# A four-layer graph network on one core: lane one-hots in two instructions, fewer TensorE signals, 15 of 98 blocks by products

## The reference

```python
m = relu(x @ Wp + bp)
agg = segment_max(m[src], dst, num_segments=n)     # 0 for a node without edges
h = x @ Ws + agg @ Wn + b                          # twice, then normalised
```

## Time and profile before

| | us |
|---|---|
| median of 3 runs (2958.58 to 2969.26) | 2963.22 |
| profiled execution | 2943.83 |
| its span | 2942.1 |

### The profile page before, as it was taken

How to read it: one execution, slowest core, us unless ns; L and a number is a source line. 1 busy time by engine, 2 the same in 40 slices (tenths; PEclk the granted TensorE clock), 3 DMA queues, 4 the chain that set the end, 5 groups by cost and what they waited for, 6 DMA issues and landing times. The chain is left out here.

```text
span 2942.1 us, 67814 instructions
## 1 busy us (share of the span) xinstructions
PE 2528.8 (86%) x26419; PEld 1892.6 (64%) x26419; DVE 1978.5 (67%) x6078; ACT 1227.1 (42%) x2920; POOL 1216.1 (41%) x1429
## 2 busy tenths in 40 slices
PE   6998999996778888747888888458799999999999
PEld 3444777773445544434455545337699999999999
DVE  7997999996788988726888888441244444444444
ACT  5997888884334444423444334330221111111110
POOL 2001999993677777634777777411000000000000
PEclk8998999997899998857999989659999999999999
DMA  6002000004343434342343444509700000000000
GB/s 197 1 1 91 12 13 12 12 12 112 93 111 107 121 109 114 104 88 68 108 120 108 112 112 137 160 8 321 239 2 2 2 2 2 2 2 2 2 2 18
DMA packets 163890, 208.87 MB, mean 71 GB/s; under 512 B 82829, under 2 KB 129194, under 8 KB 162896
## 3 DMA queue, kind: packets, MB, share of 16 engines
q1 hardware_dynamic: 135772, 165.27, 19.0%
q0 software_dynamic: 24256, 37.90, 5.3%
q10 hardware_dynamic: 3540, 1.30, 0.2%
HBM read 104.70 MB, written 102.05 MB: 70 GB/s over the span
## 5 line engine op out<-in xcount | busy, mean ns | idle before, releaser
L1782 POOL DMA_INDIRECT max_row<-table,max_src_rows x696 | 768.5, 1104 | 367.6 <-issue 240.4
L2349 PE MATMUL prop<-g,adj 128*128 128x192 f16 x9216 | 770.9, 246 | 7.1 <-PEq L2020 7.1
L2349 PEld LDWEIGHTS prop<-g,adj 128*128 128x128 f16 x9216 | 759.8, 98 | 14.9 <-issue 12.4
L1677 POOL TENSOR_SCALAR e<-e 128x512 f32<-128x512 f32 (+1 forms) x625 | 366.9, 606 | 244.4 <-ACT e L1665 228.0
L1691 DVE TENSOR_TENSOR e<-e,a_ps 128x1024 f32<-128x1024 f32 (+1 forms) x313 | 371.6, 1194 | 38.6 <-PE a_ps L1603 16.6
L2438 ACT ACTIVATE g<-prop_state 128x96 f16<-128x96 f32 (+1 forms) x375 | 106.0, 283 | 635.3 <-DVE prop_state L2406 635.3
L1665 ACT ACTIVATE e<-s_ps 128x512 f32<-128x512 f32 (+1 forms) x625 | 335.7, 585 | 62.3 <-PE o_ps L1615 38.8
L1822 PE MATMUL max_strip_ps<-max_key_hot,max_lane_w 128*128 128x400 f16 x1200 | 296.2, 361 | 72.4 <-issue 36.2
L2404 DVE SCALAR_TENSOR_TENSOR part<-prop,coef,prop_base 128x96 f32<-128x96 f32 x384 | 120.6, 314 | 312.9 <-PE prop L2349 225.5
L1875 DVE TENSOR_SCALAR max_lane_w<-iota,max_tables 128x128 f16<-128x128 f16 x1200 | 319.6, 313 | 0.0
L1812 PE MATMUL max_far<-adj 128*96 128x512 f16 x1100 | 285.9, 398 | 11.8 <-issue 11.6
(11 more groups left out here) (263 smaller groups left out, 3382.3 us busy)
## 6 DMA issues: line engine op xcount, KB each, us to landing
weights<-max_rows_w SPq DMA_DIRECT2D x52, 400.0 KB
rows_dram<-max_out SPq DMA_DIRECT2D x100, 192.0 KB
weights<-adj SPq DMA_DIRECT2D x48, 400.0 KB
ws_w<-weights SPq DMA_DIRECT2D x50, 384.0 KB, 5.2
rows_dram<-adj SPq DMA_DIRECT2D x96, 192.0 KB
ws_w<-weights SPq DMA_DIRECT2D x50, 288.0 KB, 4.5
max_row<-table,max_src_rows POOLq DMA_INDIRECT x696
ws_w<-weights SPq DMA_DIRECT2D x50, 128.0 KB, 2.8
```

What stands on the lines that cost most here:

```text
L1677: nc.gpsimd.tensor_scalar(e_tile(u), e_tile(u), math.exp(10.0), math.exp(-10.0), ALU.min, ALU.max).then_inc(clipped, 1)
L1782: nc.gpsimd.indirect_dma_start(row[i % RING][:, j, :], None, table_dram, bass.IndirectOffsetOnAxis(ap=src_rows[:, 4 * n + j:4 * n + j + 1] ...
L2349: return nc.tensor.matmul(sums(step, t), adj[:, k, t * P:(t + 1) * P], states[:, k, :], start=start and t % 2 == 0, stop=k == END - 1 and ...
```

## The change

- Far blocks: 15 of 98, every sixth, with 25 tiles over six steps and two PSUM banks in turn. `hot_used` is signalled after every second tile.
- `hots(n)`: the lane compare of all three windows is one `tensor_tensor` (384 columns), its product with both weight halves a second one (768 columns), with tables in which each lane and weight stands twice in 16 bit. Key and lane one-hots have two buffers; `hots_used` is signalled once a step.
- The low part of the strip: TensorE adds minus the high part to the strip in PSUM (`take_high`), and ScalarE copies what is left.
- `same` is loaded by SP straight from DRAM, spread over 96 partitions.
- `table` holds each row as 16-bit high and low halves (same bytes); `turn_rows` is 8 half-precision products in place of 4 float32 transposes. The layers store `table` from those halves.
- The tables are laid out by pass and loaded in one DMA.
- The count in `walk_adjacency` becomes a loop (not entered here).

```diff
-FAR = range(7, 88, 8)
+FAR = range(5, 92, 6)
@@ first_layer, second_layer: sync
-                sp.wait_ge(pooled, t + m)
-                sp.dma_start(node_view(table)[:, t:t + m, :], out[:, g % 2, 0:m, 0, :]).then_inc(stored[g % 2], 16)
                 sp.wait_ge(own_kept, t + m)
                 sp.dma_start(node_view(self_dram)[:, t:t + m, :], out[:, g % 2, 0:m, 1, :]).then_inc(stored[g % 2], 16)
+                sp.wait_ge(lo_kept, g + 1)
+                sp.dma_start(node_view(table)[:, t:t + m, :], parts[:, t:t + m, :, :].rearrange("p t a d -> p t (a d)").bitcast(F32)).then_inc(table_stored, 16)
@@ max_pass: tensor
                 for j in range(4):
-                    tr = nc.tensor.transpose(col_ps[i % 2][0:D, j * P:(j + 1) * P], row[i % RING][:, j, :], c.ident[:, :])
+                    for a in range(2):
+                        mm = nc.tensor.matmul(col_ps[i % 2][0:D, j * P:(j + 1) * P], row_parts[i % RING][:, j, a, :], c.ident16[:, :],
+                                              start=a == 0, stop=a == 1, skip_group_check=True)
...
+            def take_high(n):
+                pe.wait_ge(hi_kept, n + 1)
+                nc.tensor.matmul(strip_ps[n % 2][:, 0:KEYS], minus[:, :], strip_at(0, n).rearrange("p k d -> p d k"),
+                                 start=False, stop=True, skip_group_check=True).then_inc(hi_taken, 1)
...
-                if n >= 0 and n + SAME - 1 < NB:
-                    spread_same(n + SAME - 1)
-                for j, k in far_tiles(m):
-                    add_far(j, k)
+                tiles = far_tiles(m)
+                for i, (j, k) in enumerate(tiles):
+                    add_far(j, k, 2 if i % 2 == 1 else int(i == len(tiles) - 1))
+                if m < PARTS:
+                    take_high(m)
@@ max_pass: vector
             def hots(n):
+                steps = slice(WIN * n, WIN * (n + 1))
+                if n >= 1:
+                    dve.wait_ge(lanes_ready, n)
+                nc.vector.tensor_tensor(lane_hot.rearrange("p w (n a) -> p w n a", a=2),
+                                        c.iota16[:, 0:P].rearrange("p (n a) -> p n a", a=2).unsqueeze(1).to_broadcast([P, WIN, P // 2, 2]),
+                                        lanes[:, steps, :].unsqueeze(2).to_broadcast([P, WIN, P // 2, 2]), ALU.is_equal).then_inc(lanes_found, 1)
+                if n >= 2:
+                    dve.wait_ge(hots_used, n - 1)
                 for w in range(WIN):
...
-                    for h in range(2):
-                        one_hot = nc.vector.tensor_scalar(lane_w[:, w, h, :], c.iota16[:, 0:P], at(1), at(2 + h), ALU.is_equal, ALU.mult)
-                    one_hot.then_inc(hots_ready, 1)
+                    nc.vector.tensor_scalar(key_hot[n % 2][:, w, :], c.iota16[:, :], keys[:, WIN * n + w:WIN * n + w + 1], None, ALU.is_equal).then_inc(hots_ready, 1)
+                dve.wait_ge(lanes_found, n + 1)
+                nc.vector.tensor_tensor(lane_w[n % 2].rearrange("p h w (n a) -> p (h w) n a", a=2),
+                                        lane_hot.unsqueeze(1).to_broadcast([P, 2, WIN, P]),
+                                        weights[:, n, :, :].unsqueeze(2).to_broadcast([P, 2 * WIN, P // 2, 2]), ALU.mult).then_inc(lanes_ready, 1)
-            def low_part(n):
-                dve.wait_ge(hi_kept, n + 1)
-                nc.vector.tensor_tensor(strip_at(1, n), strip_ps[n % 2][:, 0:KEYS].rearrange("p (d k) -> p k d", d=GROUP),
-                                        strip_at(0, n), ALU.subtract).then_inc(lo_kept, 1)
@@ max_pass: scalar
+            def low_part(n):
+                act.wait_ge(hi_taken, n + 1)
+                nc.scalar.activation(strip_at(1, n), strip_ps[n % 2][:, 0:KEYS].rearrange("p (d k) -> p k d", d=GROUP), ACT.Copy).then_inc(lo_kept, 1)
@@ max_pass: sync
+            def load_same(n):
+                if n >= SAME:
+                    sp.wait_ge(scanned, n - SAME + 1)
+                at = n * BLK
+                sp.dma_start(same[n % SAME][:, :], same_dram[at:at + BLK].rearrange("(a e) -> a e", a=1).to_broadcast([D, BLK])).then_inc(same_loaded[n % SAME], 16)
```

More of the change, by code:

```diff
@@ L171, in first_layer @@
         loaded = [sem(f"loaded{g}") for g in range(len(GROUPS))]
-        stored = [sem(f"stored{i}") for i in range(2)]
+        stored, table_stored = [sem(f"stored{i}") for i in range(2)], sem("table_stored")
         w_loaded, x_stored, listed, ones_made, eps_made, d_step, x_ready, measured, std_ready, scaled = (
@@ L1700, with pass_tables, max_pass @@
 PIECES = (7, 6, 6, 6)
-def pass_tables(tables_dram, part):
-    return tables_dram.rearrange("p n (t q s) -> p n t q s", t=T, q=2)[:, :, :, part, :]
-def max_pass(nc, c, name, table_dram, src_rows, same_all, tables, rows_dram, weights_dram, part, adj, numbers, ids_dram, away_dram=None):
+PASS_STEPS = NSTEP // 2
+def pass_tables(tables):
+    keys, halves = tables[:, 0:PASS_STEPS], tables[:, PASS_STEPS:].bitcast(F16)
+    lanes = halves[:, 0:2 * PASS_STEPS].rearrange("p (s a) -> p s a", a=2)
+    weights = halves[:, 2 * PASS_STEPS:].rearrange("p (m s a) -> p m s a", s=2 * WIN, a=2)
+    return keys, lanes, weights
+def max_pass(nc, c, name, table_dram, src_rows, same_dram, tables, rows_dram, weights_dram, part, adj, numbers, minus, ids_dram, away_dram=None):
     SAME, LEAD, HOTS, OUTS = 4, 4, 6, 4
@@ L1726, in max_pass @@
         col_ps = [ps(f"col{i}") for i in range(2)]
-        back_ps, far_ps = ps("back"), ps("far")
-        same_ps = ps("same_ps")
+        back_ps, far_ps = ps("back"), [ps(f"far{i}") for i in range(2)]
         gathered = [c.gather_sem(f"{name}_gathered{i}") for i in range(RING)]
@@ L1731, in max_pass @@
         rows_stored = [sem(f"rows_stored{i}") for i in range(2)]
-        turned, cleared, scanned, spread, same_kept, back, kept, zero_out = (
-            sem("turned"), sem("cleared"), sem("scanned"), sem("spread"), sem("same_kept"),
-            sem("back"), sem("kept"), sem("zero_out"))
-        key_hot = sb("key_hot", [P, WIN, KEYS], F16)
-        lane_w = sb("lane_w", [P, WIN, 2, P], F16)
+        same_loaded = [sem(f"same_loaded{i}") for i in range(SAME)]
+        turned, cleared, scanned, back, kept, zero_out = (
+            sem("turned"), sem("cleared"), sem("scanned"), sem("back"), sem("kept"), sem("zero_out"))
+        key_hot = [sb(f"key_hot{i}", [P, WIN, KEYS], F16) for i in range(2)]
+        keys, lanes, weights = pass_tables(tables)
+        behind_out = more[:, T * P + 2 * 8 * D:]
+        lane_hot = behind_out[:, 0:WIN * P].rearrange("p (w n) -> p w n", w=WIN)
+        lane_w = [sb("lane_w", [P, 2, WIN, P], F16), behind_out[:, WIN * P:3 * WIN * P].rearrange("p (h w n) -> p h w n", h=2, w=WIN)]
+        lanes_found, lanes_ready = sem("lanes_found"), sem("lanes_ready")
         strip = sb("strip", [P, 2, T, 2, HALF], F16)
@@ L1757, in far_tiles @@
             for j, n in enumerate(FAR):
-                first, last = FAR[j - 1] + LEAD + 1 if j >= 1 else 1, n + LEAD - 1
+                first, last = FAR[j - 1] + LEAD if j >= 1 else 1, n + LEAD - 1
                 if first <= m <= last:
@@ L1843, in turn_back @@
                 tr.then_inc(back, 1)
-            for n in range(SAME - 1):
-                spread_same(n)
             for m in range(NB + LEAD):
```

146 lines of the change are left out of this document (75 added, 71 removed).

## The result

The changed kernel takes 2982.17 us (median of 7 runs, 2979.48 to 2989.74), the kernel before beside it 2967.16: the ratio is 1.0057, 95% interval 1.0041 to 1.0073. It is slower by about 15 us where 2918 was forecast. So differences between these two profiles overstate the change by about 20 us.

A forecast was written before the change was run, and what follows sets the result against it. GpSimd was taken as the bound, 490.7 of 524.2 us a pass. Own work -5 and signals -16.5 a pass, two passes -43, layer 2 -3, stores +1: -45, median 2918 us, range 2865 to 2990.

The forecast's parts named there:

- Signals: GpSimd's 33.5 us a pass of waiting for TensorE's late signals would shrink with fewer signals and doubled buffers: -16.5 us.
- Low part: Moved from VectorE to a strided TensorE product and ScalarE copy: TensorE +0.25 us a step, GpSimd -4 us a pass.
- Rival D: TensorE becomes the bound through the strided product and its wait for ScalarE, 5.5 us a step: 2979 us; chance 0.12.
- Rival A: Late TensorE signals stay, coming with full DMA engines, so only -5 us a pass: 2951 us; chance 0.20.
- Lane one-hots: On VectorE, one wide compare and one wide multiply would take 1.12 us a step in place of 1.6.
- Their weight on GpSimd: The wide lane operations on VectorE would slow GpSimd's gathers by +5 us a pass; removed lane instructions counted 0.
- Rival C: VectorE's two wide operations lock out GpSimd's gathers as far hots do: 3028 us; chance 0.10.
- Far hots: 100 more far one-hots a pass on VectorE would slow GpSimd's gathers by +14 us, between +5 and +20.8.
- GpSimd's own pass: GpSimd's gathers, issue and contention without waits would take 485.8 us a pass against 490.7.
- `same` by DMA: Loading by SP saves TensorE 0.3 us a step; the DMA share rises from 0.40 to about 0.47.
- Layer 2: The second layer would gain between 0 and 14.9 us from loading the tables in one DMA; taken -3.
- The build: A dozen more GpSimd table copies at the start, read only some 400 us later, would cost 0.

The follow-up runs named there:

- c4: Kernel before with `same` loaded by DMA alone, repeated on a late-signal chip: 0.9947 of before.
- e8: Changed kernel with 94 of 98 loads of `same` a pass left out, on a prompt chip (no late signals): 0.9866 of before.
- d1: Changed kernel with the low part back on VectorE and 11 far blocks for 15, on a prompt chip: 0.9883 of before.
- e1: Changed kernel with the low part again a subtraction on VectorE, without the product taking the high part away, on a late chip: 2963.34 us, 0.9978 of before.
- e4: Changed kernel with 11 far blocks in place of 15, on a late chip: 3007.32 us, 1.0129 of before.
- d2: d1 with rows turned by four float32 transposes in place of eight half-precision products, on a prompt chip: 0.9869 of before.
- f1: d1 once more, unchanged, on a prompt chip: 0.9854 of before.
- f2: d1 with TensorE signalling after each far tile and each window, on a prompt chip: 0.9864 of before.
- d4: Changed kernel with TensorE signalling after every far tile and every window of a strip, on a prompt chip: 0.9830 of before.

## Why the prediction was wrong

The step that failed is **Signals**: "a late signal no longer stops VectorE within the step ... I take 17: -16.5" a pass. In its own terms it came out at +29 and +33: GpSimd's waits for TensorE nearly doubled, where they were to be halved. (The profile of before was a low one, but the waits of its near copy `c4`, 40 and 42 us in the profile's terms, are the same.) What the runs show in its place has two parts. First, fewer signals don't make GpSimd wait less. With 679 for 958 the lateness at ScalarE's high part did fall, about as their number, from 79 to 55 us; at the scans, for which TensorE's next turns of rows wait in the program, it rose from 48 to 83. Second, the buffers were doubled for VectorE, while the product that takes the high part away put a new round trip, TensorE to ScalarE and back within a step, into TensorE's own queue, where TensorE stands 57 and 54 us a pass. Changing its read, moving it or taking it away gives back 17 to 25 us. That is shown by the times, on two chips for the read. That this is by way of the late signals is argued: GpSimd's waits don't fall with it, and without the product they are 92 and 94 us. So the product is enough to explain that the kernel is 15 us slower, but not the growth of the waits, whose cause stays open.

**Low part**: 0.25 us of TensorE was taken with 0.47 as the end; the step timeline has 0.66, 831 ns on the record, so TensorE's quiet step is 4.76 and not 4.25. The nearest row, a float32 turn, wasn't near in what counts: there the read was dense, here every column lies 256 B from the last. Reading in runs of 16 makes it 0.30 us, 520 ns on the record.

**Rival D** named this product and this wait and gave 2979, three microseconds off, which is in part luck: it had 5.5 us a step for TensorE, and the quiet step is 4.76. Its story is half of it: undoing it on a late chip ends at 0.997 to 0.998 of before, so all that the change saves elsewhere (25 us a pass of GpSimd's own) is still not collected. On a prompt chip the wait is short (`e8` has 9.5 us of TensorE idle before it in two passes); what the product costs there was not taken by itself, since `d1` without it also has 11 blocks. **Rival A**, late signals stay, is the other half; it gave 2951 because it let them stay at 33.5. Its sign, ScalarE still 6 us late, didn't come: the longest at the high part is 4.5 us.

**Lane one-hots**: compare and multiply take 0.329 + 0.545 = 0.87 us; 1.12 was taken, 0.73 to 1.52 were the ends. The estimate from the Trainium skill's rate ("VectorE: DVE Perf Modes", the perf-mode tier table) was 0.92, and the trace agrees with it. **Their weight on GpSimd**, taken +5 a pass with nothing for the lanes that go, is about -20 ((1.112 - 1.054) x 348). The 57 us of contention had been given "mostly" to the far hots, from two rows of a timeline; by `d1` some 20 of them went with the six narrow instructions a step that this change takes away. Rival C is refuted on every chip: no gathers' mean is over 1.15 us, where its sign was 1.25. The Trainium skill's rule against it ("SBUF — State Buffer", *Who interferes with whom*) is that an operation with two SBUF inputs blocks GpSimd only where GpSimd reads SBUF; the fall to 1.054 us agrees with it in direction. **Far hots** were taken at +14. With the product they cost 20 to 30 on prompt chips, about the end of +20.8; but `e1`, with all 375 of them and without the product, has gathers of 1.052 us on a late chip, as short as those of `d1` with 275. So their price by themselves isn't known. The errors left GpSimd's own pass at 466 to 482 on prompt chips, where 485.8 was forecast for it.

**Smaller ones**: `same` by DMA, taken as nearly free, is a gain of 13 to 16 us on a late chip and none on a prompt one. Layer 2 was to gain 3 and lost 2 (from its first gather to pass 2's 83.3 us for 81.2; 82.6 to 83.3 in all relatives on late chips). The build, taken at 0, had the first gather 2.9 us later, which is within the spread of profiles (718.7 in the repeat of the changed kernel, 719.6 in before).

**The size of it all**: -45 us, or 1.5%, was forecast; relatives of the change measure -1.2 to -1.7% on prompt chips. The changed kernel itself was not run on one. The forecast read the trace of a late chip, saw the lateness, and treated it as a leftover that shrinks with the number of signals.

**Open**: why signals are late on some chips at all; and what makes GpSimd's waits grow from 41 to 93 (with the product undone). `same` by DMA doesn't (`c4`), nor do the 15 blocks by themselves (`e4`, with the product); left are the one-hots, the row products and the fewer signals. The kernels made for that (`d1`, `d2`, `f1`, `f2`) ran on prompt chips only. No one version is best on both kinds: 0.9947 is before with `same` by DMA (late chip), 0.9830 is `d4` (prompt chip), and neither was run where the other wins, but for the first, 1.0007 on a prompt chip.

## What to carry to other kernels

Don't put into an engine's in-order queue a step that needs another engine's answer to a signal of the same step, unless independent work stands between them, at best as long as the signal delays seen in the trace; here such a step cost 17 to 25 us of 2967. Price a strided read by a row with that stride, or measure it alone; here it was better to read in stored order and let the PSUM write take the stride. Take a measure of delay at more than one engine, and trust it only as far as the bounding engine's waits and the time move with it: with the change it rose at one place and fell at another, and in `c4` it rose at both while the time fell. And when waits in a profile have no cause in the program, run the kernel on more than one chip before promising what they will give back.

## What the runs showed of the hardware

The same program takes 2964 to 2969 us on some chips and 2833 to 2840 on others. In the passes the difference shows as consumers of TensorE's semaphores starting up to 11 us after its instructions ended, also with a DMA share of 0.14, while the product that takes the high part away (831 and 832 ns) and the gathers (1.107 and 1.112 us) take the same on both. The kernel before with `same` by DMA was profiled on both kinds. Its two passes from first to last gather are 527 and 525 us against 492 and 493, which is 66 of the 120 us between the profiles; 19 more lie in the second layer (81.7 against 63.0) and 17 behind the third layer's first gather. The mean granted clock was 0.911 against 0.925.

A float16 product of 400 columns costs TensorE 0.2 us dense, 0.66 where each column lies 256 B further (831 ns on the record), and 0.30 (520 ns on the record) with runs of 32 B and a strided PSUM write.

A gather's mean went from 1.112 to 1.054 us when 600 narrow float16 instructions with scalar operands on VectorE a pass became 200 wide ones with two tensors, beside the rest of `d1`'s edits.
